# A new order of the units on all four engines, and one score row cut at another column, in an attention and mixture-of-experts layer

## The reference

```python
x = L0_attn_h                     # (2, 1024, 256)
xn = _layernorm(x, axis=-1)
x = x + attn(xn, ...) + ffn(xn, ...)

# attn: a second layernorm with gain and bias, 16 heads of 128, rotary positions, causal softmax
q = (z @ wq.T + bq).reshape(b, s, 16, 128); k = ...; v = ...
q = rope(q); k = rope(k)
attn = jnp.where(causal, -jnp.inf, jnp.einsum('bihd,bjhd->bhij', q, k) * scale)
attn = jax.nn.softmax(attn, axis=-1)
o = jnp.einsum('bhij,bjhd->bihd', attn, v).reshape(b, s, 2048)
return o @ wo.T + bo + residual

# ffn: a router over 32 experts (4 groups of 8, best 2 groups, best 4 experts), 64 slots per expert
scores = jax.nn.sigmoid(x @ gate_w.T); sc = scores + gate_bias
...
h = jax.nn.silu(einsum(buf, w1)) * einsum(buf, w3); ob = einsum(h, w2)
...
shared = jax.nn.silu(x @ shared_gate) * (x @ shared_up) @ shared_down
return (out + shared)
```

## Time and profile before

| | before |
|---|---|
| median of 3 runs (lowest to highest) | 1061.93 us (1060.56 to 1063.89) |
| the profiled execution's own time | 1061.38 us |
| its span | 1059.5 us |
| PE busy | 1022.0 us (96%), 6500 instructions |
| DVE busy | 726.5 us (69%) |
| ACT busy | 659.0 us (62%) |
| POOL busy | 749.8 us (71%) |
| HBM read and written | 33.94 MB and 10.90 MB |

### The profile page before, as it was taken

How to read it: one execution, slowest core, us unless ns; L and a number is a source line. 1 busy time by engine, 2 the same in 40 slices (tenths; PEclk the granted TensorE clock), 3 DMA queues, 4 the chain that set the end, 5 groups by cost and what they waited for, 6 DMA issues and landing times.

```text
span 1059.5 us, 18814 instructions
## 1 busy us (share of the span) xinstructions
PE 1022.0 (96%) x6500; PEld 915.8 (86%) x6500; DVE 726.5 (69%) x1747; ACT 659.0 (62%) x1450; POOL 749.8 (71%) x654
## 2 busy tenths in 40 slices
PE   3999999999998999999999999999999999999997
PEld 3898888888887888888998989998988989999896
DVE  6867778877789766766666666666666666665667
ACT  4566665656665666666665666756576665666663
POOL 4825776777676575787778697877878778787770
PEclk9999999999999999999999999999999999999999
DMA  7211326212221221323232323323223322231232
GB/s 237 61 57 40 93 67 124 65 27 46 50 61 36 40 46 41 64 69 83 53 97 71 79 69 88 98 46 80 71 74 95 84 73 63 66 80 29 43 100 80
DMA packets 51629, 75.42 MB, mean 71 GB/s; under 512 B 12240, under 2 KB 29008, under 8 KB 51408
## 3 DMA queue, kind: packets, MB, share of 16 engines
q1 hardware_dynamic: 46144, 67.66, 24.1%
q0 software_dynamic: 5392, 6.56, 3.9%
HBM read 33.94 MB, written 10.90 MB: 42 GB/s over the span
## 4 chain that ended last, share of the span: by engine, by line
PE 81%; DVE 6%; POOL 6%; ACT 3%; DMA 2%; issue 1%; SPq 0%; DVEq 0%; POOLq 0%; ACTq 0%
PE ps L294 23%; PE ps L296 22%; PE ps L295 22%; PE ps L417 9%; PE ps L500 2%; DMA qs<-qb 2%; POOL qb L1586 1%; POOL qb L1582 1%; POOL qs L1583 1%; DVE ps L1435 1%; PE ps L512 1%; DVE acc L1475 1%; POOL q_l L1115 1%; ACT prob L994 1%; PE ps L326 0%
## 5 line engine op out<-in xcount | busy, mean ns | idle before, releaser
L1582 POOL TENSOR_TENSOR qb<-qb,k_sb 128x512 f32<-128x512 f32 x128 | 170.3, 1331 | 221.6 <-DMA qs<-qb 221.0
L1435 DVE CUSTOM_DVE_ANT_0 ps<-ps,maskr 128x128 f32<-128x128 f32 (+7 forms) x256 | 193.7, 763 | 56.7 <-PE ps L296 56.3
L994 ACT ACTIVATE prob<-ps,nmax 128x128 f32<-128x128 f32 (+7 forms) x256 | 190.3, 743 | 62.6 <-DVE nmax L1435 60.8
L1005 ACT ACTIVATE ptd_h<-ps 128x128 fp32r<-128x128 f32 (+3 forms) x256 | 108.6, 436 | 171.9 <-PE ps L417 170.9
L1586 POOL TENSOR_TENSOR qb<-qb,qs 128x512 f32<-128x512 f32 x128 | 165.6, 1294 | 19.0 <-POOL qs L1583 1.0
L1445 DVE TENSOR_TENSOR ptd_l<-ps,ptd_h 128x128 fp32r<-128x128 f32 (+3 forms) x256 | 124.6, 487 | 79.1 <-ACT ptd_h L1005 75.3
L417 PE MATMUL ps<-k_sb,prob 128*128 128x128 f32 x1152 | 171.9, 273 | 2.1 <-ACT prob L994 1.0
L1583 POOL TENSOR_TENSOR qs<-qs,k_sb 128x512 f32<-128x512 f32 x128 | 171.7, 1341 | 0.0
L417 PEld LDWEIGHTS ps<-k_sb,prob 128*128 128x128 f32 x1152 | 135.6, 141 | 18.3 <-issue 2.7
L294 PE MATMUL ps<-k_h,q_h 128*128 128x512 f32 (+3 forms) x384 | 141.1, 367 | 3.3 <-ACT prob L994 2.4
L296 PE MATMUL ps<-k_h,q_l 128*128 128x512 f32 (+3 forms) x384 | 132.9, 346 | 0.0
(11 more groups left out here) (178 smaller groups left out, 2613.4 us busy)
## 6 DMA issues: line engine op xcount, KB each, us to landing
qs<-qb SPq DMA_DIRECT2D x256, 128.0 KB
ew<-epack SPq DMA_DIRECT2D x16, 768.0 KB, 4.3
rqk<-wqk SPq DMA_DIRECT2D x16, 256.0 KB, 2.9
xt<-x SPq DMA_DIRECT2D x4, 512.0 KB, 4.7
rv<-wvp SPq DMA_DIRECT2D x8, 256.0 KB, 3.3
ro<-wop SPq DMA_DIRECT2D x16, 128.0 KB, 2.3
token_table<-xn SPq DMA_DIRECT2D x4, 512.0 KB, 4.8
token_sum<-token_table SPq DMA_DIRECT2D x1, 2048.0 KB, 9.4
```

Of the source, the lines that this page charges most:

```text
L994: act.activation(prob[:, t % 2, 0:w], score[t % 2][:, 0:w], ACT.Exp, bias=nmax[:, t:t + 1], scale=-1.0, accum_out=rsum[:, t:t + 1]).then_i ...
L1005: act.activation(turned(0, t, j0, w), src, ACT.Copy).then_inc(pth_done, 1)
L1435: dve.tensor_tensor_reduce(out=score[t % 2][:, 0:w], in0=score[t % 2][:, 0:w], in1=maskr[:, SEQ - w:SEQ], scale=-1.0, scalar=3e38, op0=ALU ...
L1582: pool.tensor_tensor(qb[:, i, :], qb[:, i, :], cos_sb[:, c], ALU.mult).then_inc(rope_a, 1)
```

## The change

The loops that write the order are rewritten on all four engines, and three things beside it change. First, the score row of tile 4 is placed at column 128 of its buffer and is cut at the bank's border there: 384 + 256 columns in place of 512 + 128 (`tile[4]`, `mid`). DVE and ACT use the same place. Second, the transposes of a unit stand in five groups (turns 10, 11 and the next unit's 0; 1 and 2; 3 to 5; 6 and 7; 8 and 9), and the late output's last part, outproj(.,1,1), is done a unit later than the first, at the start of unit n for unit n-2. `recips` gets a wait for the additions that still read the buffer it writes. Third, the three router steps of a unit stand together behind maxes(n,1), before maxes(n,3), and the late steps are given to other units: the scan to unit 9, the two finds to units 10 and 11. On POOL the gather moves behind the next unit's first rope, rope_lo(.,2) as well, and the second scatter to the end of its turn.

```diff
+        tile = [score[t % 2][:, P * (t == 4):P * (t == 4) + (t + 1) * P] for t in range(TILES)]
...
-                dst, i = score[t % 2], slice(t * P, (t + 1) * P)
+                dst, i = tile[t], slice(t * P, (t + 1) * P)
+                mid = CH - P * (t == 4)
                 for c in range(t // 4 + 1):
-                    w = min(CH, (t + 1) * P - c * CH)
-                    j = slice(c * CH, c * CH + w)
+                    j = slice(c * mid, min((t + 1) * P, mid + c * CH))
                     ins = three(pe, dst[:, j], (q_h[s][:, i], q_l[s][:, i]), (k_h[s][:, j], k_l[s][:, j]), True, True)
...
 
             for n in range(UNITS):
                 scores(n, 0)
-                turn(n - 1, 8)
-                turn(n - 1, 9)
                 if n > 1:
                     values(n - 1, 2)
-                scores(n, 1)
                 if n > 1:
                     values(n - 1, 3)
+                outproj(n - 2, 1, 1)
+                project(n + 1, 1)
+                outproj(n - 1, 0, 0)
+                scores(n, 1)
                 turn(n - 1, 10)
-                expert_down(n - 1)
                 turn(n - 1, 11)
-                project(n + 1, 1)
+                turn(n, 0)
                 scores(n, 2)
                 masks(n, 0)
                 bias_row(n)
-                outproj(n - 1, 0, 0)
-                outproj(n - 1, 0, 1)
-                turn(n, 0)
-                turn(n, 1)
+                expert_down(n - 1)
+                project(n + 1, 2)
+                weighted(n - 1, 1, range(4))
                 scores(n, 3)
                 masks(n, 1)
-                weighted(n - 1, 1, range(4))
-                turn(n, 2)
                 weighted(n - 1, 1, range(4, 8))
                 expert_turn(n)
+                turn(n, 1)
+                turn(n, 2)
                 scores(n, 4)
-                project(n + 1, 2)
-                turn(n, 3)
                 project(n + 1, 3)
                 scores(n, 5)
-                outproj(n - 1, 1, 0)
+                masks(n, 2)
+                turn(n, 3)
                 turn(n, 4)
-                scores(n, 6)
-                outproj(n - 1, 1, 1)
+                turn(n, 5)
                 if n:
                     values(n, 0)
-                expert_up(n)
                 if n:
                     values(n, 1)
-                turn(n, 5)
-                project(n + 2, 0)
-                scores(n, 7)
+                outproj(n - 1, 0, 1)
+                scores(n, 6)
+                masks(n, 3)
+                weighted(n, 0, range(4))
                 turn(n, 6)
                 turn(n, 7)
-                weighted(n, 0, range(4))
+                expert_up(n)
+                project(n + 2, 0)
+                outproj(n - 1, 1, 0)
+                if n == UNITS - 1:
+                    outproj(n - 1, 1, 1)
+                scores(n, 7)
+                turn(n, 8)
+                turn(n, 9)
 
             u = UNITS - 1
-            turn(u, 8)
-            turn(u, 9)
             outproj(u, 0, 0)
             outproj(u, 0, 1)
             weighted_part(u, 0)
...
-                elif k == 3 * MASKS + 1:
+                elif k == 3 * (MASKS + 1):
                     route_scan()
-                elif k == 3 * MASKS + 2:
+                elif k == 3 * (MASKS + 2):
                     route_find(0)
-                elif k == 3 * MASKS + 3:
+                elif k == 3 * (MASKS + 3):
                     route_find(1)
-                elif k == 3 * MASKS + 4:
+                elif k == 3 * (MASKS + 3) + 1:
                     route_take()
...
             def recips(n, c):
                 dve.wait_ge(exp_done, TILES * n + 4 * c + 4)
+                if n:
+                    dve.wait_ge(add_done, 4 * (n - 1) + 2 * c + 2)
...
                 if n == 1:
                     dve.memset(ones[:, :], 1.0).then_inc(ones_ready, 1)
                 maxes(n, 0)
+                turned_lo(n - 1, 9)
                 if n > 1:
                     v_lo(dve, n - 1, 2)
-                maxes(n, 1)
                 if n > 1:
                     v_lo(dve, n - 1, 3)
+                add_out(n - 2, 1, 1)
+                add_out(n - 1, 0, 0)
                 turned_lo(n - 1, 10)
                 turned_lo(n - 1, 11)
-                add_out(n - 1, 0, 0)
+                maxes(n, 1)
+                route(n, 0)
+                maxes(n, 2)
+                recips(n - 1, 1)
+                route(n, 1)
                 turned_lo(n, 0)
-                maxes(n, 2)
-                add_out(n - 1, 0, 1)
+                route(n, 2)
                 maxes(n, 3)
-                route(n, 0)
-                turned_lo(n, 1)
-                recips(n - 1, 1)
-                expert_copy(n)
-                turned_lo(n, 2)
-                recips(n, 0)
                 out_lo(n - 1, 1)
                 maxes(n, 4)
-                route(n, 1)
-                turned_lo(n, 3)
+                expert_copy(n)
+                turned_lo(n, 1)
+                turned_lo(n, 2)
...
             for m in range(1, UNITS):
                 base(m)
                 rope(pool, m, 0)
+                gather(m - 1)
+                if m > 1:
+                    rope_lo(pool, m - 1, 2)
                 if m > 1:
                     rope_lo(pool, m - 1, 3)
                 scatter(m - 2, 0)
@@ -1669,12 +1683,11 @@
                 if m == 1:
                     pool.wait_ge(rope_l, 4)
                 rope_lo(pool, m, 0)
-                scatter(m - 2, 1)
                 rope(pool, m, 2)
                 rope_lo(pool, m, 1)
-                gather(m)
                 rope(pool, m, 3)
-                rope_lo(pool, m, 2)
+                scatter(m - 2, 1)
+            rope_lo(pool, UNITS - 1, 2)
             rope_lo(pool, UNITS - 1, 3)
             pool.wait_ge(cb_done, 1)
             for q in range(NG):
```

107 lines of the change are left out of this document (56 added, 51 removed).

## The result

| | before | changed kernel |
|---|---|---|
| median of 5 runs (lowest to highest) | 1060.56 us (1059.61 to 1063.89) | 1069.74 us (1067.47 to 1073.17) |
| ratio, 95% interval | | 1.0082 [1.0056, 1.0108] |
| profiled execution, its span | 1061.38, 1059.5 us | 1067.47, 1065.6 us |
| DVE busy | 726.5 us | 761.4 us |
| DVE's share of the chain that ended last | 6% | 16% |

The medians alone give a ratio of 1.0087. The profiled execution of the changed kernel is its fastest one, so what is read from its trace explains 6.1 us (1065.6 less 1059.5) of a difference of some 9.

The account below looks back on a forecast made before the run. PE was taken to bound the kernel, its idle time to 460 us mostly delays handed on by DVE. From 1061.4 us, -4.8 + 0 - 12 + 1 - 0.5 = -16.3 gave 1045.1, so 1045.5 us; range 1038 to 1056.

Parts of the forecast that it names:

- Step 1: PE's scores of tile 4, cut 384 + 256 for 512 + 128: 0.15 us in 32 units, -4.8 us (-4.2 to -5.4).
- Step 2: PE's transposes in five groups in place of eight: fewer changes of kind are worth 0 us (bounds +0.5 and -1.5).
- the joints: Weighted rows ending in a 128 wide triple, now followed by transposes, may escape 0.05 us each; lower bound -1.5 us.
- Step 3: DVE's router steps bunched and additions moved away from them, removing PE's waits up to 460 us: -12 us (0 to -14).
- Step 4: New hand-overs: project(n+1,3) in 16 expert units may wait for its PSUM bank: +1 us (0 to +3).
- the ring of PSUM banks: Four PSUM banks used in turn; project(n+1,3) reuses that of the weighted values of c=1, with 0.1 us to spare.
- The end: Last unit: the wait for `ol` goes, additions behind maxes(.,7) bring some 1.5 us of waits: -0.5 us (+-1.5).
- The slower one: Rival: ACT or DVE reaches the weighted PSUM bank late, each of 16 expert units waits: 1068 us, chance 0.08.
- The signs named as wrong: Waits before project(n+1,3) naming `ol` over 0.3 us, or scores(n,5) waiting for `prob` above 2 us summed, units 1 to 9.

Follow-up runs that it names:

- the kernel with two places: Changed kernel, weights' low parts behind turned_lo(n,4) to unit 12, then between maxes(n,3) and out_lo(n-1,1), value weights' at next unit's start: 1051.68 us, ratio 0.9908.

## Why the prediction was wrong, step by step

**The bound** was read rightly: PE bound, and the waits for `acc` up to 460 us were a delay that DVE hands on. "Nearly all" of the idle time was too much, since 6.9 of 10.7 us is two thirds. With the low parts out of the way 0.8 us of waits for `acc` is left up to 460 us, of 2.1 idle.

**Step 1**, the cut. Right in kind and sign. Scores 4 in the changed kernel are a 384 triple of 0.60 behind transposes and a 256 triple of 0.36 (534.82, 535.42 and 535.78), as forecast, and the joint behind costs 0.01 in place of 0.05. The term was -4.8 and measured -2.8 alone and -2.9 in the new order: both below the lower bound of 4.2, though the first one's interval reaches 4.1. The pitch of an undisturbed unit shows the forecast 0.15; the profiled execution of the cut alone shows units in which it is taken back, but no run isolates why.

**Step 2**, the joints, 0. The nine transposes take 0.90 us (538.22 to 539.12), 0.10 each, and the matmul behind them 0.08 more than its own pace. An undisturbed unit before the experts went from 28.40 to 28.20 us, 0.15 of which is the cut. So 0.05 per unit may be for the joints, within the bounds.

**Step 3**, the router's steps and the additions. Forecast -12. The bunching alone measured 9.4 (with the low parts moved) and 10.5 (in the changed kernel's own order, from 1.0082 to 1.0181). For the whole step there is the span of units 0 to 12 in the kernel with two places: 11.4 us shorter than before, of which the cut alone has 1.1, so 10.3. The mechanism held, the size was too large by some 2 us. Unit 0 was called even at +-1: units 0 and 1 together went from 45.6 to 46.8 us, with a new wait of 2.42 us and behind it, from 98 to 104 us, a granted clock of 0.70 and 0.73; moving unit 0's steps away did not shorten the kernel.

**Step 4**, new hand-overs, +1. This is the step that failed. It followed the ring of PSUM banks of project(n+1,3), and there it was right: no wait of 0.2 us or more stands there. The only wait for `ol` between 460 and 1020 us stands before another use of the ring, project(n+2,0), late in unit 19:

```profile
674.02 0.47 PE L296 MATMUL ps<-x2h,wqh 128*128 128x512 f32 x1 [0.91 <-DVE ol L1466]
```

It never asked what DVE does between a transpose and the weighted values that read its low part. The calls of the weights' low parts are unchanged lines of the kernel, but turned_lo(n,3) moved from ahead of them to behind them and behind maxes(n,5), and on PE weighted(n,0) and values(n,1) wait for it. With the durations of before this puts 0.7 to 1.5 us of low parts and 1.0 us of maxes(n,5) in front of it, a sum that the prediction could have made. And the step took for granted that an instruction keeps its duration when it is moved. The kernel before shows that it need not: the mean of `wol` was 486 ns, but one in its trace, beside a busy POOL, took 1.51 us:

```profile
332.58 1.51 DVE L1142 TENSOR_TENSOR wol<-ro,woh 128x256 fp32r<-128x256 f32 x1
```

Where +1 was forecast, moving these instructions to two other places gave 18 us (1069.74 to 1051.68), more than the whole forecast of 16.3.
How much of that is the place and how much the lengthening is only partly shown. The lengthening is 32.8 us of DVE time; 7.9 us taken away at that place were worth some 8 us. The other way round, low parts that stayed long (61.0 us) behind turned_lo(n,4) no longer made PE wait for turned_lo(n,3), but up to unit 30 that was worth 3.2 us in units 0 to 12 and 0.4 in the others. The old durations at the place that the change gave them were not run.
The Trainium skill (SBUF — State Buffer, section Who interferes with whom) has the rule for it: a DVE instruction with two SBUF inputs contends with a GpSimd instruction that reads SBUF, and the ports that the two share are an exclusive lock, so the one that comes second is blocked. The runs agree: 1.32 us for 92 columns beside POOL's 1.35, 0.61 unchanged with an input in PSUM.

**The end**, -0.5: measured +1.6 (41.0 to 42.6 us from unit 31), within 0.1 the same in every kernel with the new order but the one with POOL's old order (44.2). The forecast gain is there: the wait of 1.02 us for `ol` is gone. The additions behind maxes(31,7) cost waits of 0.86 and 0.39 us, near the 1.5 that the text had named. What it had not named are waits for `ptd_l` of 0.94 and 1.06 us, and the second is step 4's error once more: an addition of 1024 columns now stands ahead of turned_lo(31,3), and beside a busy POOL it takes 2.46 us in place of 1.22.

**The rivals.** The slower one named another place (the bank of step 4) with a similar mechanism and the same time, 1068: an engine that reaches a thing late in each unit. That the times agree is luck: the bank it named made no wait. Its chance of 0.08 was far too low, since it was the chance of one bank, when the new order made many new pairs of producer and reader per unit and only one had been followed. The signs named as wrong (`ol` above 0.3, `prob` above 2 us in units 1 to 9) did not show either: the wait named `ptd_l`.

**The sum from measured sizes:** cut -2.8, router's steps -9.4, end +1.6, which gives -10.6; the kernel with the low parts at two places measured -10.1. That they meet is partly chance, since the sum leaves out two things that cancel in the table above: step 3 as a whole is nearer 10.3, and units 13 to 30 take 557.9 us where the cut alone has 555.5, so some 2.4 us of small new waits are left there. The changed kernel lies 18.1 us above this one by the medians, and by the ratios 18.5 (0.9908 to 1.0082).

## What to carry to other kernels

When an order is rewritten, go through every reader on the bounding engine and ask of each what now stands ahead of its input's producer in the producer's queue, above all rare instructions (each kind in every fourth unit) that no diff shows as moved because only their neighbours moved. A duration belongs to a place: look in the trace of before whether the same instruction has a slow form, and what the other engines did then. A gain in one stage and a loss in another cancel in the total, so a change should be tried part by part: here one idea was worth -9 us and a detail of the same new order +18.

## What the runs showed of the hardware

- VectorE and GpSimd exclude each other in some instructions on SBUF operands: 0.61 us becomes 1.68 (subtraction, two f32 inputs), 0.35 becomes 1.40 (f32 copy and bf16 subtraction), GpSimd's product 1.23 becomes 1.62; an input in PSUM takes the f32 subtraction out of it (0.61). A narrow instruction does not help (92 columns: 1.32), starting between two of GpSimd's does (0.24). The profile shows all this as busy time, not as a wait.
- Short waits can cost several times their length. In the kernel with the low parts behind turned_lo(n,4), 0.89 and 0.37 us of idle PE were followed by a granted clock near half speed and a unit 3.6 us longer. But it doesn't follow each time. The kernel before waits 1.92 and 1.08 us at 336 us, and the clock stayed at full speed there; with the cut alone it fell to 0.50 from 336 to 339 us, behind a wait of 2.08 us at the same place. Unit 0's wait of 2.4 us was followed by 0.70 and 0.73 in the changed kernel and by 1.00 in the kernel with two places. What decides it no run here shows.
